# Stacked attention rows: four rows a channel in scratch memory, loaded by one transfer a side in lines of 2 KB

## The chip, the cores and the metric

The kernel runs on one NeuronCore of a Trainium2 chip. The metric is the device time of one execution in microseconds (us). Before the change the median of three runs is 694.81 us (693.26 to 694.91).

## What is computed

A decoder layer over x of 4 batches x 512 tokens x 256 channels, in float32. Only the first part is touched by the change:

```
x = layernorm(x + causal self-attention(x))     # 16 heads of 16 channels, weights 256 x 256
x = layernorm(x + cross-attention(x, ctx))      # 16 heads of 64 channels, 64 context rows a batch
x = layernorm(x + experts(x))                   # 8 experts, top 2, 256 -> 1024 -> 256
```

Self-attention: q = x Wq + bq, k = x Wk + bk, scores = q k / 4 with a causal mask, softmax, times v, times Wo, plus bo.

## The kernel before

**Precision by stacking.** Matmuls take float16. To keep float32 precision q and k are each split into a high and a low part (`qk[:, hl]`), and q k is formed as high x high + high x low + low x high. For that each channel is stacked as three rows of the contraction: `PARTS` says which part (0 high, 1 low) stands in row m on the q side and on the k side. A head has 16 channels, so 48 rows. Heads go in 8 pairs; the even head of a pair lies in partitions 0 to 47 and the odd one in partitions 64 to 111 of `qs` and `ks` (128 partitions x 8 pairs x 512 tokens). Row 48 (and 112) of `qs` holds minus the row maximum of the scores against ones in `ks`, so the score matmul (64 rows, `ROWS`) comes out with the maximum taken off; the rest of the 64 rows is zero in `qs`.

**Who fills the stacks.** For batch 0 TensorE stamps the rows out of `qk` with a 0/1 matrix `stamp` (step `st`, L926), and ScalarE evicts them (L618, L619). For batches 1, 2 and 3 the stacks go through scratch memory in HBM: step `store` (L437) writes six transfers of 256 KB, one for each side and row m, each a 1 KB line (one channel, 512 tokens) per descriptor. Step `stack` (L448) reads it back with four transfers of 384 KB: for each of `qs` and `ks` and each half of a pair 48 partitions x 8 pairs, again in lines of 1 KB, with the 8 lines of one partition 96 KB apart. Each batch has its own region of scratch. `qs` and `ks` have two buffers, batch b uses b % 2.

**Order.** All engines walk one handwritten list of steps, `ORDER`, in this order, each taking the steps that are its own; inside a batch the numbers are b:n. SyncE (SP) issues all these transfers from one queue. For batch b: `ql:b:1` (the low part of k is done) lets `store:b:0` go; `stack:b:0` waits for `qk_stored` and for the last score matmul of batch b-2; `m:b:0` on TensorE waits for `stack_in`. Steps `m:b:0` to `m:b:21` compute all scores once (L225, with the causal mask added by L230) for VectorE to take row maxima (L240); then `mT` and `max` bring the maxima into `qs` (L456), and `s:b:n` (L1035) computes the scores again for the exponentials (L681, ScalarE), `w` the sums with v (L1049), `ct`, `ct.n`, `cx`, `o` the projection, with VectorE's `cx.l` (L720), `o.d` (L817, then moments at L727 and L731), GpSimd's `r` (L559, L562) and VectorE's `n` (L828) for the layernorm. The `m` steps of batch b+1 are interleaved with the `s` and `w` steps of batch b and with the cross-attention (`xa`, `S`, `T`, `O`) of batch b. The part of the list around the second load reads:

```
o:0:0 o.d:0:0 stack:2:0 r:0:0 s:1:3 o:0:1 o.d:0:1 m:2:0 r:0:1 vw:0:0 w:1:0 ax:0:0 n:0:0 s:1:4 m:2:1 n:0:1 x1b:0:0 w:1:1 m:2:2 xa:0:0
```

Steps `A.s` and `VW.s` store products of the cross-attention's weights (`stage`) in scratch, also from SP's queue; `fold_done` waits for all of them, on ScalarE and VectorE ahead of `cx:0:0`, on SP ahead of the loads of `a_x` (L481) and `vw` (L488), 1 MB each.

Of the kernel before, what the change touches and what calls it, by code (L numbers as in the profile page):

```python
# [61 lines left out]
XS = 16.0  # L62
QS = 4.0
NEG = -60000.0
STACK = 3 * HD
PARTS = ((0, 0, 1), (0, 1, 0))
STORES, LOADS = 6, 4
ROWS = 64

# [118 lines left out]
class Tally:  # L190
# [3 lines left out]

    def upto(self, *step):
        return self.place[step]


def flat(ap):
# [44 lines left out]
def attention_block(nc, ctx, dram, keep):  # L244
# [100 lines left out]

    def kinds_of(x, hl):

        at = [m for m in range(3) if PARTS[x][m] == hl]
        step = at[1] - at[0] if len(at) > 1 else 1
        return stamp[:, x, hl, :].rearrange("p (r e) -> p r e", r=2)[:, :, 0:STACK].rearrange(  # L350
            "p r (d m) -> p r d m", m=3)[:, :, :, at[0]:at[-1] + 1:step], len(at)

    def fold_done(eng):

# [18 lines left out]
    def diagonal(n, hl, par):  # L373

        rows, pairs = slice(64 * par, 64 * par + 64), slice(n % 2 * 4, n % 2 * 4 + 4)
        return rows, v_diag[rows, hl, pairs, :, par, :].rearrange("p k b n -> p (k b) n")

    def half_of(n, hl):
        return pT[:, n // 2 % 2, hl, n % 2 * 4:n % 2 * 4 + 4, :].rearrange("p k q -> p (k q)")
# [10 lines left out]
    @block.sync  # L390
    def _(sp):
        def tokens(b, dst, done):
            sp.dma_start(dst[:, :, :], dram["x"][b * S:b * S + S, :]
                         .rearrange("(t p) d -> p t d", p=128)).then_inc(done, 16)

        tokens(0, x_tok, x_in)
        for n, w in enumerate(("Wq", "Wk")):
            sp.dma_start(w_f[:, n, :, :], dram[w].rearrange("(c p) n -> p c n", p=128)).then_inc(w_in[0], 16)
        sp.dma_start(qk_bias[:, 0, :], dram["bq"]).then_inc(b_in, 16)
        sp.dma_start(qk_bias[:, 1, :], dram["bk"]).then_inc(b_in, 16)  # L400
        for n, w in enumerate(("Wv", "Wo")):
            sp.dma_start(w_f[:, 2 + n, :, :], dram[w].rearrange("(c p) n -> p c n", p=128)).then_inc(w_in[1], 16)

        def load_rest():
            rows = dram["cond"].rearrange("(t p) d -> p t d", p=128)
            sp.dma_start(cond[:, :, 0, :], rows[:, :, 0:128]).then_inc(c_in, 16)
            for par in range(2):
                sp.dma_start(cond[:, :, 1, 64 * par:64 * par + 64], rows[:, :, 128:DCOND]).then_inc(c_in, 16)
            for n, w in enumerate(("w_k", "w_v")):
                sp.dma_start(wkv_f[:, n, :], dram[w][0:128, :]).then_inc(wkv_in[n], 16)  # L410
                sp.dma_start(wkv_f[64 * n:64 * n + 64, 2, :], dram[w][128:DCOND, :]).then_inc(wkv_in[2], 16)
            for n, bias in enumerate(("bo", "bv", "b_out")):
                sp.dma_start(b_rows[:, n, :], dram[bias].partition_broadcast(128)).then_inc(r_in, 16)
            sp.dma_start(wq_f[:, :, :], dram["w_q"].rearrange("(c p) n -> p c n", p=128)).then_inc(wq_in, 16)
            sp.dma_start(wout_f[:, :, :], dram["w_out"].rearrange("(k p) n -> p k n", p=128)).then_inc(wo_in, 16)
            sp.dma_start(wg_f[:, :, :], dram["WgT"]).then_inc(wg_in, 16)

        for kind, b, n in STEPS:
            if kind == "x_in":
                filled(sp, g, "xT", b - 1, 1)  # L420
                tokens(b, x_tok, x_in)
                if b == 1:
                    load_rest()
            elif kind == "xr_in":
                if b == 0:
                    sp.wait_ge(wout_lo, 1)
                    for m in range(4):
                        freed_slot(sp, r, "kv", m, 0)
                else:
                    freed_slot(sp, g, "o", b - 1, 1)  # L430
                tokens(b, x_res, xr_in)
            elif kind == "store":
                sp.wait_ge(qlo_done, 2 * b + 2)
                rows = dram["qk"][b * 6 * D:(b + 1) * 6 * D, :].rearrange("(t c p m) s -> t m p c s", t=2, c=DC, m=3)
                for t, parts in enumerate(PARTS):
                    for m, hl in enumerate(parts):
                        sp.dma_start(rows[t, m, :, :, :], qk[:, hl, 2 * t:2 * t + 2, :]).then_inc(qk_stored, 16)  # L437
            elif kind == "stack":

                sp.wait_ge(qk_stored, STORES * 16 * b)  # L440
                if b < 2:
                    sp.wait_ge(stack_set, 2)
                else:
                    filled(sp, r, "s", b - 2, STAGE - 1)
                rows = dram["qk"][b * 6 * D:(b + 1) * 6 * D, :].rearrange("(t p r e) s -> t r e p s", t=2, r=2, e=STACK)
                for t, dst in enumerate((qs[b % 2], ks[b % 2])):
                    for par in range(2):
                        sp.dma_start(dst[64 * par:64 * par + STACK, :, :], rows[t, par, :, :, :]).then_inc(stack_in[b % 2], 16)  # L448
            elif kind == "max":

                freed_slot(sp, g, "mT", b, 0)
                if b >= 2:
                    sp.wait_ge(stack_in[b % 2], (b + 1) // 2 * LOADS * 16)
                for par in range(2):
                    row = 64 * par + STACK
                    sp.dma_start(qs[b % 2][row:row + 1, :, :], neg_maxT[par * PAIRS:(par + 1) * PAIRS, :]  # L456
                                 ).then_inc(max_in, 16)
            elif kind == "A.s":
                use = use_of["A", b]
                sp.wait_ge(a_lo, b + 1)  # L460
                c, q = b // 4, b % 4
                dst = dram["ax"].rearrange("(b p) (l c n) -> p l b c n", p=128, l=2, c=DC)[
                    :, :, :, c, q * 256:q * 256 + 256]
                src = stage[:, use % 2, :, :].rearrange("p l (b n) -> p l b n", b=NB)
                for hl in range(2):
                    sp.dma_start(dst[:, hl, :, :], src[:, hl, :, :]).then_inc(staged[use % 2], 16)
            elif kind == "VW.s":
                use = use_of["VW", b]
                freed_slot(sp, r, "VW", b, 0)
                half = b % 2  # L470
                dst = dram["vw"][b // 2 * 128:b // 2 * 128 + 128, :].rearrange("p (l h n) -> p l h n", l=2, h=2)[
                    :, :, half:half + 1, :]
                src = stage[:, use % 2, :, :].rearrange("p l (h n) -> p l h n", h=1)
                for hl in range(2):
                    sp.dma_start(dst[:, hl, :, :], src[:, hl, :, :]).then_inc(staged[use % 2], 16)
            elif kind == "ax":
                if b == 0:
                    fold_done(sp)
                else:
                    filled(sp, g, "S", b - 1, 2 * NQ - 1)  # L480
                sp.dma_start(a_x[:, :, :, :].rearrange("p l c n -> p (l c n)"),  # L481
                             dram["ax"][b * 128:b * 128 + 128, :]).then_inc(ax_in, 16)
            elif kind == "vw":
                if b == 0:
                    fold_done(sp)
                else:
                    filled(sp, g, "O", b - 1, NQ - 1)
                sp.dma_start(vw[:, :, :, :].rearrange("p l k n -> p (l k n)"),  # L488
                             dram["vw"][b * 128:b * 128 + 128, :]).then_inc(vw_in, 16)
        sp.wait_ge(wg_lo, 1)  # L490
# [91 lines left out]
    def _(act):  # L582
# [7 lines left out]
        for kind, b, n in STEPS:  # L590
# [7 lines left out]
            elif kind == "q":  # L598
                if b == 0 and n == 0:
                    act.wait_ge(bias_done, 2)  # L600
                if n == 0 and b > 0:
                    positive(act, qk_stored, STORES * 16 * (b - 1))
                bank, empty = filled(act, r, kind, b, n)

                if b > 0:
# [100 lines left out]
    def _(dve):  # L706
# [16 lines left out]
        def moments(n, buf):  # L723
# [6 lines left out]
            for t in tiles:  # L730
# [3 lines left out]
        dve.wait_ge(consts, 1)  # L734
        V.tensor_reduce(squares[:, :], ident[:, :].rearrange("p (j e) -> p e j", e=32), AX.X, ALU.add
                        ).then_inc(squares_sum, 1)
        V.tensor_reduce(pads[:, :], ident[:, :].rearrange("p (r e) -> p r e", r=2)[:, :, STACK:], AX.XY, ALU.add
                        ).then_inc(pads_set, 1)
        dve.wait_ge(squares_sum, 1)
        dve.wait_ge(stamp_clear, 1)  # L740
# [145 lines left out]
    def _(pe):  # L886
# [15 lines left out]
        for kind, b, n in STEPS:  # L902
# [14 lines left out]
            elif kind == "st":  # L917
# [2 lines left out]
                    pe.wait_ge(stamp_set, 4)  # L920
                    pe.wait_ge(qlo_done, 2)
                bank, full = opened(r, kind, b, n)
                rows = slice(32 * (n % 4), 32 * (n % 4) + 32)
                for x in range(2):
                    for hl in range(2):
                        last = M.matmul(bank[:, x, :], stamp[rows, x, hl, :], qk[rows, hl, 2 * x + n // 4, :],  # L926
                                        start=hl == 0, stop=hl == 1)
                last.then_inc(full, 1)
            elif kind == "v":
# [97 lines left out]
            elif kind == "s":  # L1027
# [1 line left out]
                    pe.wait_ge(max_in, 32 * b + 32)  # L1029
                bank, full = opened(r, kind, b, n)  # L1030
                for x, j, at in SCORES[n % ITEMS]:
                    p = 2 * (n // ITEMS) + x
                    for par in range(2):
                        rows = slice(64 * par, 64 * par + ROWS)
                        last = M.matmul(bank[:, par, at:at + S - 128 * j], ks[b % 2][rows, p, 128 * j:128 * j + 128],  # L1035
# [830 lines left out]
```

## Time and profile before

| | |
|---|---|
| median of 3 runs | 694.81 us |
| the profiled execution's own time | 693.73 us |
| its span | 692.0 us |
| mean granted TensorE clock | 0.969 |
| busy: PE, DVE, ACT, POOL | 603.4, 530.1, 407.9, 303.2 us |
| attention block | up to about 412 us of the span |
| transfers from SP's queue | 92.55 MB |

PE is TensorE's matmuls, PEld its weight loads (they overlap), DVE is VectorE, ACT ScalarE, POOL GpSimd, SPq the queue of SyncE. "L225" is a line of the kernel. "idle before <-releaser" says how long an engine sat idle just ahead of an instruction and whose work ended that wait. A busy PE is not a PE at its peak, since ends of matmuls are modelled; idle time of an engine that is not the one everything waits for costs nothing.

### The profile page before, as it was taken

Reading aid. Unit: us, or ns where it says so; the run is one execution under the profiler, and the core shown is the slowest. Engines: PE = TensorE matmul, PEld = TensorE weight load, DVE = VectorE, ACT = ScalarE, POOL = GpSimd, SP = SyncE. Lnnn points to the kernel's source line nnn. Section 1 sums busy time; section 2 is a strip of 40 time slices with the busy share of each in tenths; the row PEclk is TensorE's granted clock in tenths of the full one; section 3 lists DMA queues with packets and bytes.
Section 4 is the critical chain, followed back from the end, with each engine's and each line's share of the span. In section 5 each row is a group of like instructions: output and inputs, shape, how many; then the busy total and the mean of one; then the engine's idle time right before and its main releaser. Section 6 shows DMA issues by size and latency. Waiting matters only on the chain. (4 is left out here: it accounts for less than half of the span.)

```text
span 692.0 us, 13570 instructions
## 1 busy us (share of the span) xinstructions
PE 603.4 (87%) x5232; PEld 414.6 (60%) x5232; DVE 530.1 (77%) x930; ACT 407.9 (59%) x622; POOL 303.2 (44%) x363
## 2 busy tenths in 40 slices
PE   5989688887999799898987853899999999999984
PEld 2435344453444535454654543698989989988963
DVE  4687576528877688877757779699999999999725
ACT  3655578763466344455651313388888988987613
POOL 9311255545356244625452434325464642662223
PEclk9999999999999999999999995699999999999998
DMA  7407454394002900111020017578888779786264
GB/s 229 143 1 176 100 153 153 104 254 163 1 1 92 218 28 14 48 64 31 1 94 30 0 35 239 169 260 267 300 288 283 264 267 290 264 279 208 92 227 161
DMA packets 70992, 103.65 MB, mean 150 GB/s; under 512 B 4848, under 2 KB 56776, under 8 KB 69904
## 3 DMA queue, kind: packets, MB, share of 16 engines
q1 hardware_dynamic: 67184, 92.55, 42.3%
q0 software_dynamic: 3744, 10.23, 4.2%
q8 instruction: 42, 0.69, 0.4%
q14 instruction: 22, 0.18, 0.1%
HBM read 80.28 MB, written 22.41 MB: 148 GB/s over the span
## 5 line engine op out<-in xcount | busy, mean ns | idle before, releaser
L240 DVE TENSOR_REDUCE rowmax<-M 128x1 f32<-128x512 f32 (+3 forms) x176 | 104.6, 636 | 37.6 <-PE M L230 35.5
L681 ACT ACTIVATE probs<-R 128x1024 f32<-128x1024 f32 x80 | 80.4, 1028 | 51.2 <-PE R L1035 50.9
L213 PE MATMUL HB<-xT,w 128*128 128x256 f16 (+1 forms) x1104 | 107.8, 258 | 0.3 <-DVE xT L1615 0.3
L1770 PE MATMUL YB<-w,h 128*128 128x256 f16 x936 | 105.9, 273 | 0.1
L213 PEld LDWEIGHTS HB<-xT,w 128*128 128x128 f16 x1104 | 94.8, 98 | 11.2 <-DVE xT L1615 1.7
L1770 PEld LDWEIGHTS YB<-w,h 128*128 128x128 f16 x936 | 91.4, 98 | 10.8 <-issue 0.4
L543 POOL TENSOR_SCALAR_AFFINE_SELECT probs<-probs 128x256 f32<-128x256 f32 x128 | 49.6, 407 | 97.4 <-ACT probs L681 96.9
L1467 ACT ACTIVATE hf<-HB,b 128x256 f32<-128x256 f32 (+1 forms) x184 | 69.9, 445 | 37.0 <-PE HB L213 35.5
L1388 POOL DMA_INDIRECT scratch_ys<-y,dst x39 | 41.9, 1075 | 98.2 <-ACT y L1447 93.0
L1380 POOL DMA_INDIRECT xg<-scratch_xs,src x39 | 62.4, 1601 | 26.6 <-issue 10.9
L1642 DVE SCALAR_TENSOR_TENSOR h<-hf,h 128x512 f16<-128x512 f32 (+1 forms) x92 | 56.6, 616 | 3.2
L1627 DVE SCALAR_TENSOR_TENSOR w<-w2f,w 128x2048 f16<-128x2048 f32 x23 | 52.6, 2288 | 8.3 <-ACT w L1453 8.3
L225 PE MATMUL M<-ks,qs 48*128 48x384 f16 (+3 forms) x256 | 33.8, 303 | 21.0 <-DVE rowmax L240 13.7
L1620 DVE SCALAR_TENSOR_TENSOR w<-w1f,w 128x2048 f16<-128x2048 f32 x22 | 50.3, 2285 | 1.0 <-ACT w L1438 0.6
L213 PE MATMUL M<-a_x,x1T 128*128 128x512 f16 x192 | 45.6, 380 | 5.0 <-DVE logits L874 1.6
L213 PE MATMUL M<-vw,pT 128*128 128x256 f16 x384 | 44.6, 273 | 3.2 <-DVE pT L720 3.1
L1438 ACT ACTIVATE w<-w1f 128x2048 f16<-128x2048 f32 x23 | 44.2, 1920 | 4.1 <-DMA w1f<-in_W 4.1
L1453 ACT ACTIVATE w<-w2f 128x2048 f16<-128x2048 f32 x23 | 44.3, 1927 | 2.2 <-DMA w2f<-in_W 2.2
L1049 PE MATMUL PV<-probs,v_aug 128*32 128x256 f32 (+3 forms) x512 | 44.2, 444 | 0.0
L213 PEld LDWEIGHTS M<-vw,pT 128*128 128x128 f16 x384 | 36.7, 98 | 10.9 <-DVE pT L720 4.3
L578 POOL TENSOR_TENSOR e_x<-e_x,xinv 128x1024 f32<-128x1024 f32 x16 | 30.4, 1902 | 22.4 <-DVE xinv L852 22.3
L225 PEld LDWEIGHTS M<-ks,qs 48*128 48x128 f16 x256 | 12.1, 95 | 43.8 <-issue 23.8
(272 smaller groups left out, 1071.7 us busy)
## 6 DMA issues: line engine op xcount, KB each, us to landing
w1f<-in_W SPq DMA_DIRECT2D x23, 1024.0 KB, 7.6
w2f<-in_W SPq DMA_DIRECT2D x23, 1024.0 KB, 6.0
scratch_qk<-qk SPq DMA_DIRECT2D x18, 256.0 KB, 3.0
scratch_ax<-stage SPq DMA_DIRECT2D x16, 256.0 KB, 2.5
scratch_vw<-stage SPq DMA_DIRECT2D x16, 256.0 KB, 2.9
vw<-scratch_vw SPq DMA_DIRECT2D x4, 1024.0 KB, 7.4
a_x<-scratch_ax SPq DMA_DIRECT2D x4, 1024.0 KB, 9.5
parts<-scratch_ys SPq DMA_DIRECT2D x8, 512.0 KB, 8.6
```

The source lines that it names most:

```text
L213: last = nc.tensor.matmul(out, left(a, k), right(b, k), start=(k == 0 and m == 0), stop=(k == n - 1 and m == 2))
L225: nc.tensor.matmul(banks[par][:, p * wide:p * wide + wide], qs[rows, p0 + p, t * 128:t * 128 + 128], ks[rows, p0 + p, 0:wide], start=p == ...
L240: return nc.vector.tensor_reduce(rowmax[:, t, par * PAIRS + p0:par * PAIRS + p0 + pairs], bank[:, 0:pairs * wide].rearrange("p (n w) -> p ...
L543: last = P.affine_select(out=diag, in_=diag, compare_op=ALU.is_ge, fill=0.0, base=0, pattern=[[0, 2], [1, 128]], channel_multiplier=-1)
L681: A.activation(probs[:, n % RING, :, :], bank[:, :, :], ACT.Exp, scale=1.0 / (QS * QS)).then_inc(empty, 1)
L1380: pool.indirect_dma_start(out=xg[:, n % 2, t, :], out_offset=None, in_=dram["xs"], in_offset=bass.IndirectOffsetOnAxis(src[:, at:at + 1], ...
L1453: A.activation(w2[:, q, 0, :, :].rearrange("p m d -> p (m d)"), w2f[:, q, :, :].rearrange("p m d -> p (m d)"), ACT.Copy, scale=WS).then_in ...
L1467: last = A.activation(hf[:, 2 * b + m, 0:width(n)], HB[b][:, m, 0:width(n)], ACT.Gelu, bias=b1[:, 2 * b + m, WORK[n]:WORK[n] + 1], scale=1 ...
L1620: V.scalar_tensor_tensor(w1[:, q, 1, :, :].rearrange("p c f -> p (c f)"), w1f[:, q, :, :].rearrange("p c f -> p (c f)"), WS, w1[:, q, 0, : ...
L1627: V.scalar_tensor_tensor(w2[:, q, 1, :, :].rearrange("p m d -> p (m d)"), w2f[:, q, :, :].rearrange("p m d -> p (m d)"), WS, w2[:, q, 0, : ...
L1642: V.scalar_tensor_tensor(h[:, q, 1, pair, at], hf[:, pair, at], XS, h[:, q, 0, pair, at], ALU.mult, ALU.subtract).then_inc(h_split, 1)
L1770: last = M.matmul(YB[q][:, t, :], h[:, q, a, m, t * 128:t * 128 + 128], w2[:, q, b, m, :], start=((m, a, b) == (0, 0, 0)), stop=((m, a) == ...
```

## The change

Each channel now has four rows in scratch, of which the fourth is a filler (zeros for q, ones for k, written once ahead of the first store from the set buffers `qs[1]` and `ks[1]`). `STACK` and `ROWS` are 64, so a head fills its half of the partitions. The two chunks c of 128 channels lie side by side, so that a line is 2 KB. One region of scratch serves all batches, so a store waits until the load of the batch before has landed. A store is four transfers (two of them write a part twice, from a source with a step of zero), a load is two transfers of 1 MB, over all 128 partitions, with the 4 lines of one partition 256 KB apart. Pairs take another order (`place_of`), and minus the maximum goes to row 3 (and 67). The stamps and pads of batch 0 follow the new order of rows.

```diff
-STACK = 3 * HD
+PARTED = 4
+STACK = PARTED * HD
-STORES, LOADS = 6, 4
-ROWS = 64
+STORES, LOADS = 4, 2
+ROWS = STACK
...
+def places(x, hl):
+    at = [m for m in range(3) if PARTS[x][m] == hl]
+    return slice(at[0], at[-1] + 1, at[-1] - at[0] or 1), len(at)
...
+    def place_of(pair):
+        return pair % (PAIRS // DC) * DC + pair // (PAIRS // DC)
...
+        stack_rows = dram["qk"].rearrange("(t p m c) s -> t p m (c s)", t=2, m=PARTED, c=DC)
+        stack_lines = dram["qk"].rearrange("(t q e c) s -> t e q (c s)", t=2, e=128, c=DC)
...
                 sp.wait_ge(qlo_done, 2 * b + 2)
-                rows = dram["qk"][b * 6 * D:(b + 1) * 6 * D, :].rearrange("(t c p m) s -> t m p c s", t=2, c=DC, m=3)
-                for t, parts in enumerate(PARTS):
-                    for m, hl in enumerate(parts):
-                        sp.dma_start(rows[t, m, :, :, :], qk[:, hl, 2 * t:2 * t + 2, :]).then_inc(qk_stored, 16)
+                if b == 1:
+                    sp.wait_ge(stack_set, 2)
+                    for t, fill in enumerate((qs[1], ks[1])):
+                        sp.dma_start(stack_rows[t, :, 3, :], flat(fill[:, 0:DC, :])).then_inc(qk_stored, 16)
+                else:
+                    sp.wait_ge(stack_in[(b - 1) % 2], b // 2 * LOADS * 16)
+                for t in range(2):
+                    for hl in range(2):
+                        where, many = places(t, hl)
+                        sp.dma_start(stack_rows[t, :, where, :], flat(qk[:, hl, 2 * t:2 * t + 2, :]).unsqueeze(1)
+                                     .to_broadcast([128, many, DC * S])).then_inc(qk_stored, 16)
...
-                sp.wait_ge(qk_stored, STORES * 16 * b)
+                sp.wait_ge(qk_stored, (2 + STORES * b) * 16)
...
-                rows = dram["qk"][b * 6 * D:(b + 1) * 6 * D, :].rearrange("(t p r e) s -> t r e p s", t=2, r=2, e=STACK)
                 for t, dst in enumerate((qs[b % 2], ks[b % 2])):
-                    for par in range(2):
-                        sp.dma_start(dst[64 * par:64 * par + STACK, :, :], rows[t, par, :, :, :]).then_inc(stack_in[b % 2], 16)
+                    sp.dma_start(dst[:, :, :].rearrange("e (q c) s -> e q (c s)", c=DC), stack_lines[t, :, :, :]
+                                 ).then_inc(stack_in[b % 2], 16)
...
-                    row = 64 * par + STACK
+                    row = 64 * par + PARTED - 1
...
-                    positive(act, qk_stored, STORES * 16 * (b - 1))
+                    positive(act, qk_stored, (2 + STORES * (b - 1)) * 16 if b > 1 else 0)
...
-                rows = slice(32 * (n % 4), 32 * (n % 4) + 32)
+                rows, c = slice(32 * (n // DC), 32 * (n // DC) + 32), n % DC
...
-                    p = 2 * (n // ITEMS) + x
+                    p = place_of(2 * (n // ITEMS) + x)
```

## Rows read from the trace of the kernel before

**Rows 1.** Busy time by stretch: us, engines (instructions), clock, DMA share, GB/s.
```profile
159.00:216.00 57.00, 52.59 (x418) 24.98 (x418) 46.63 (x84) 30.32 (x41) 27.32 (x35) 1.00 0.09 37
239.00:300.00 61.00, 55.51 (x458) 27.08 (x456) 52.70 (x95) 28.97 (x36) 28.60 (x41) 0.97 0.13 48
```

**Rows 2.** Waits of the whole span: us in total, times, longest.
```profile
PE M L225 <- DVE rowmax L240: 13.7, 22, 1.0
PE M L225 <- DMA ks<-scratch_qk: 6.5, 2, 3.9
```

**Rows 3.** Timeline ahead of and behind the load of batch 2: start, duration.
```profile
146.88 0.96 SPq L448 DMA_DIRECT2D qs<-scratch_qk  x2
158.09 0.25 DVE L731 BATCH_NORM_AGGREGATE meanvar<-stats 128x2 f32<-128x6 f32 x2
158.92 0.40 PE L225 MATMUL M<-ks,qs 48*128 48x128 f16 x8 [2.57 <-DMA ks<-scratch_qk]
159.67 1.29 DVE L240 TENSOR_REDUCE rowmax<-M 128x4 f32<-128x512 f32 x2 [1.34 <-PE M L230]
```

**Rows 4.** Timeline around the load of batch 3.
```profile
226.20 0.90 SPq L448 DMA_DIRECT2D qs<-scratch_qk  x2
236.22 0.25 DVE L731 BATCH_NORM_AGGREGATE meanvar<-stats 128x2 f32<-128x6 f32 x2
238.74 0.40 PE L225 MATMUL M<-ks,qs 48*128 48x128 f16 x8 [3.95 <-DMA ks<-scratch_qk]
239.49 1.29 DVE L240 TENSOR_REDUCE rowmax<-M 128x4 f32<-128x512 f32 x2 [3.02 <-PE M L230]
241.73 1.29 DVE L240 TENSOR_REDUCE rowmax<-M 128x4 f32<-128x512 f32 x2 [0.30 <-PE M L230]
244.29 1.29 DVE L240 TENSOR_REDUCE rowmax<-M 128x2 f32<-128x512 f32 x2 [0.62 <-PE M L230]
```

**Rows 5.** Stretches behind that wait (columns as Rows 1): the granted clock.
```profile
239.00:240.00 1.00, 1.00 (x12) 0.27 (x8) 0.51 (x1) 0.00 (x0) 0.00 (x0) 0.73 1.03 434
241.00:242.00 1.00, 1.00 (x6) 0.13 (x2) 0.70 (x3) 1.00 (x2) 0.47 (x2) 0.50 0.95 393
242.00:243.00 1.00, 1.00 (x9) 0.20 (x8) 1.00 (x3) 0.28 (x1) 0.85 (x3) 0.57 1.01 363
```

**Rows 6.** Pace of transfers by stretch (columns as Rows 1, the last is GB/s).
```profile
148.40:156.00 7.60, 5.43 (x42) 3.38 (x43) 2.75 (x6) 3.60 (x5) 3.67 (x5) 1.00 1.10 201
227.20:236.00 8.80, 7.59 (x67) 6.03 (x65) 5.67 (x16) 3.67 (x4) 2.18 (x5) 1.00 1.09 178
22.00:24.00 2.00, 1.52 (x9) 0.42 (x7) 1.38 (x2) 1.17 (x2) 0.00 (x0) 1.00 1.07 382
238.00:241.00 3.00, 2.26 (x26) 1.21 (x26) 1.51 (x3) 0.66 (x1) 0.00 (x0) 0.74 0.99 418
138.20:142.50 4.30, 4.30 (x46) 2.14 (x46) 0.69 (x3) 3.60 (x7) 2.70 (x3) 1.00 1.07 352
147.00:148.20 1.20, 1.10 (x10) 0.86 (x8) 0.27 (x2) 1.20 (x3) 0.00 (x0) 1.00 1.17 372
```

**Rows 7.** Issues in 226 to 228: queue, count, KB each, median us to landing.
```profile
qs<-scratch_qk SPq DMA_DIRECT2D x2, 384.0 KB, 5.6
ks<-scratch_qk SPq DMA_DIRECT2D x2, 384.0 KB, 9.7
```

**Rows 8.** Timeline of SP's stores and of what waits for the last of them.
```profile
137.89 3.82 SPq L437 DMA_DIRECT2D scratch_qk<-qk  x6
144.13 1.22 DVE L720 SCALAR_TENSOR_TENSOR stage<-R,stage 128x1024 f16<-128x1024 f32 x1 [4.67 <-ACT stage L667]
145.79 1.00 SPq L475 DMA_DIRECT2D scratch_vw<-stage  x2
151.02 1.08 ACT L588 ACTIVATE ctxT<-M 128x512 f16<-128x512 f32 x2 [2.04 <-DMA scratch_vw<-stage]
```

**Rows 9.** Timeline of batch 1: load issued, first matmul on it.
```profile
63.76 0.99 SPq L448 DMA_DIRECT2D ks<-scratch_qk  x2
82.56 0.32 PEld L225 LDWEIGHTS M<-ks,qs 48*128 48x128 f16 x8
```

**Rows 10.** Matmuls on the stacks by form, 48 and 64 rows: count, busy, mean ns.
```profile
L225 PE MATMUL M<-ks,qs 48*128 48x512 f16 x64 | 12.8, 382 | 5.9 <-DVE rowmax L240 5.9
L1035 PE MATMUL R<-qs,ks 64*128 64x512 f16 x64 | 12.3, 386 | 2.3 <-DVE stage L720 1.4 <-ACT w_f L663 0.5 <-ACT v_next L623 0.2
```

More of the change, by code:

```diff
@@ L346, in kinds_of @@
     def kinds_of(x, hl):
[L348 to L351, printed above, removed]
+        where, many = places(x, hl)
+        return stamp[:, x, hl, :].rearrange("p (r d m) -> p r d m", r=2, m=PARTED)[:, :, :, where], many
     def fold_done(eng):
@@ L736, in _ @@
                         ).then_inc(squares_sum, 1)
-        V.tensor_reduce(pads[:, :], ident[:, :].rearrange("p (r e) -> p r e", r=2)[:, :, STACK:], AX.XY, ALU.add
+        V.tensor_reduce(pads[:, :], ident[:, :].rearrange("p (d m) -> p d m", m=PARTED)[:, :, PARTED - 1:], AX.XY, ALU.add
                         ).then_inc(pads_set, 1)
@@ L922, in _ @@
                 bank, full = opened(r, kind, b, n)
-                rows = slice(32 * (n % 4), 32 * (n % 4) + 32)
+                rows, c = slice(32 * (n // DC), 32 * (n // DC) + 32), n % DC
                 for x in range(2):
                     for hl in range(2):
-                        last = M.matmul(bank[:, x, :], stamp[rows, x, hl, :], qk[rows, hl, 2 * x + n // 4, :],
+                        last = M.matmul(bank[:, x, :], stamp[rows, x, hl, :], qk[rows, hl, 2 * x + c, :],
                                         start=hl == 0, stop=hl == 1)
@@ L1858 @@
     dram["out"] = nc.dram_tensor("out", (T, D), F32, kind="ExternalOutput").ap()
-    for name, shape, dt in (("qk", (NB * 6 * D, S), F16), ("ax", (NB * 128, 2 * DC * XA), F16),
+    for name, shape, dt in (("qk", (2 * PARTED * D, S), F16), ("ax", (NB * 128, 2 * DC * XA), F16),
                             ("vw", (NB * 128, 2 * PAIRS * D), F16),
```

## Prediction

> **What bounds the kernel now.** I read the busy times by stretch first. Between the load of batch 2 and that of batch 3, and behind the latter, TensorE is busy 52.59 of 57 us and 55.51 of 61 us, VectorE 46.63 and 52.70 [rows 1]. TensorE works through one list in order, so what it idles there moves the end unless another engine holds it up anyway. The list of waits names the two causes: 13.7 us in 22 small waits for row maxima, and 6.5 us in only two waits for the transfer into `ks` [rows 2]. The timeline shows both: 2.57 us ahead of `m:2:0` [rows 3] and 3.95 us ahead of `m:3:0` [rows 4]. VectorE sits idle behind them, but less, as it still has the moments of a layernorm to do: 1.34 us and 3.02 us [rows 3, 4]. The clock rows show one more cost: after the 3.95 us idle the granted clock falls from 1.0 to one half, from 2.4 to 1.2 GHz, for about 3.4 us (0.54 of the 239th, the next two, and 0.86 of the 242nd) [rows 5]. Nothing of the sort follows on the 2.57 us one.
>
> Why is the load late? It moves 4 x 384 KB = 1.57 MB. With all DMA engines busy (share 1.09 to 1.10) the queue makes only 201 and 178 GB/s in the two stretches that it fills, while 1 KB lines of `w_out` to 128 partitions, 128 KB apart, go at 382, and the 8 KB lines of `a_x` and `vw` at 418 [rows 6]. So 1 KB lines are not slow as such. What sets this load apart is that a transfer reaches 48 partitions of one half.
>
> **The load, changed.** Two transfers over 128 partitions in 2 KB lines carry 2 x 1,048,576 B = 2.10 MB, a third more. At the pace of the nearest row of like shape, 382 GB/s, that is 5.5 us; at 418 it is 5.0; at the old 178 it is 11.8. I take 5.5.
>
> Batch 3: the first transfer is issued at 226.20 and the data flow from 227.2. At 178 GB/s 1.57 MB last 8.8 us, to 236.0. The last `ks` transfer lands just before TensorE starts at 238.74, at about 238.65: that leaves a tail of 2.6 us for what `a_x` and `vw` take of the engines and for the completion. The median landing of the two `ks` transfers, 9.7 us against 5.6 for `qs`, shows the queue growing [rows 4, 6, 7]. New: 227.2 + 5.5 + 2.6 = 235.3. TensorE is there at 238.74 - 3.95 = 234.79 and waits 0.5 us at most. VectorE ends its moments at 236.47, and needs the result of `m:3:0` 0.75 us after its start (239.49 against 238.74), so at 235.3 + 0.75 = 236.05 it is in time. VectorE gains its whole idle time, 3.02 us.
>
> Batch 2: stores are still in the queue when the load is issued at 146.88 (372 GB/s from 147.0 to 148.2), so I start at 148.3: 148.3 + 5.5 + 2.6 = 156.4, against 156.35 when TensorE is there and 158.34 - 0.75 = 157.6 when VectorE needs it [rows 3, 6]. It gains 1.34 us.
>
> Which of the engines' gains goes on? Ahead of `xa`, TensorE needs both halves of the layernorm (`n`), and these stand on VectorE behind the row maxima of `m:b:0` and `m:b:1`. So VectorE's gain passes, and the rest of TensorE's becomes waits for row maxima. I take 1.34 + 3.02 = 4.36 us. The upper end is TensorE's own 2.57 + 3.95 = 6.52 us.
>
> **The clock.** With TensorE idle for 0.5 us in place of 3.95 I expect no fall there. VectorE waited 0.30 and 0.62 us for matmuls at the low clock [rows 4]: 0.92 us, which I take. The upper end is half of the 3.4 us at low clock, 1.7 us; the lower is none, if the fall comes somewhere else.
>
> **The stores.** Six transfers become four, of the same 1.57 MB, in 768 lines of 2 KB instead of 1,536 of 1 KB. They go at 352 GB/s now [rows 6], 4.5 us; at the 372 of the stores of `vw`, which have lines of 2 KB, 4.2. SP spends 3.82 us on six issues, 0.64 each, so about 1.3 less. That matters at one place: `VW.s:7:0` is issued at 145.79, 0.44 after VectorE is done at 145.35, and ScalarE waits 2.04 us for its landing ahead of `ctxT`, on whose path the layernorm of batch 0 stands [rows 8]. I take 0.4 us, between -0.5 (2 KB lines of the load get among the last stores) and 1.9 (TensorE's wait for `ctxT` gone). The wait added ahead of the store, for the load of the batch before, would hold up SP's queue, that is `max`, `A.s`, `VW.s` and `stack` behind it, and with them `s` and `m` of TensorE. It costs nothing: the loads of batches 1 and 2 are in use from 82.56 and 158.92, the stores of 2 and 3 come at 137.89 and 58 us after the second [rows 3, 8, 9]. The two filler transfers (0.52 MB, 1.5 us at 352) delay only the load of batch 1, issued by 64.75 and landed some 10 us later, if it takes what the `ks` transfers of rows 7 take, but wanted at 82.56 [rows 9]: over 7 us of cover, and the load gets shorter.
>
> **Matmuls.** `m` goes from 48 to 64 rows. 48 rows take 382 ns and 64 rows 386 at 512 columns [rows 10]; the 4 ns may be a matter of place. 64 x 4 ns = 0.26 us, bounds 0 and 0.3: I take 0.1. The order of pairs, row 3 for the maximum, stamps and pads change addresses only: nothing, with bounds of 0.2 either way, as the instructions keep their shapes.
>
> **Sum.** -4.36 - 0.92 - 0.4 + 0.1 = -5.6 us. Against the profiled execution's own time of 693.73: 688.1. Against the median, 694.81, it would be 689.2; the two differ by 1.1 us, which is the spread of the runs. I predict 688.6 us, which is 5.6 below 694.2; the rivals' times are from 694.2 too. The part from 300 us on is left as it is; it starts earlier.
>
> **Rivals.**
> 1. *The source is what is slow* (slower). The load reads back what was just written, in lines far apart. If this sets 178 to 201 GB/s, and not the 48 partitions, then 2.10 MB take 11.8 us in batch 3 and 10.4 in batch 2: 3.0 and 2.6 us longer than 1.57 MB now. Both waits grow by that, and the one of 5.2 us at `m:2:0` brings a low clock too, some 1 us: +6.6, 701 us. It decides below 2.10 / 8.8 = 238 GB/s, the pace at which the new load lasts as long as the old. For it: the data come from scratch, and lines 96 KB apart become lines 256 KB apart. Against it: lines 128 KB apart at 382, and `vw` and `a_x`, also from scratch, at 418 [rows 6]. [...]
> 2. *Half a gain* (no change). The pace comes out near 280 GB/s, between 178 and 382: 7.5 us. Batch 3 lands at 227.2 + 7.5 + 2.6 = 237.3 and gains 1.35, batch 2 at 158.4 gains 0.5, and the low clock may stay: 1.9 us or less, 692.3.
> 3. *TensorE's whole wait comes back.* If row maxima are not what holds it afterwards, 6.52 + 1.7 and 0.4 of the stores make -8.6: 685.6. Against it: 13.7 us of waits for row maxima as it is [rows 2].
>
> **How the numbers follow.** Forecast 0.66, rival 3 0.12, rival 2 0.12, rival 1 0.10. A run is told from no change beyond 0.3%, 2.1 us. The forecast and rival 3 are faster, and a little of rival 2: 0.79. Same: 0.13. Slower: 0.08, as a mild form of rival 1 stays within 2.1 us. The forecast's own range is 686 to 691. The whole range is 685.3 to 693.5: it holds rivals 2 and 3 and leaves out rival 1.
>
> **What would show it.** The list of waits has no wait for `ks` above 1 us. The two loads show 350 GB/s or more and land within 10 us of issue; at 238 or less rival 1 holds. The clock stays at 1.0 behind `m:3:0`. `xa:0:0` starts some 1.7 us and `xa:1:0` some 5.5 us earlier than now, while the small waits for row maxima grow by 1 to 2 us. If the load is early and the end is not, my step from VectorE's idle time to the end was wrong.

## The result, and the profile after

| | median us | runs | lowest, highest |
|---|---|---|---|
| before | 697.14 | 12 | 693.26, 711.63 |
| after | 689.73 | 12 | 685.24, 695.78 |

The ratio is 0.9891, 95% interval 0.9859 to 0.9923: the kernel is faster by 7.6 us (5.4 to 9.8). The forecast of 688.6 us was a gain of 5.6, a ratio of 0.992, inside the interval, near its upper end. Ratios, here and below, leave out the runs that lie over 1.5% above the fastest of their kernel, so they differ a little from those of the medians.

The profiled execution of the changed kernel has a span of 694.0 us (own time 695.78), 2 us longer than that of before. In it, as in some of those below, TensorE was granted a lower clock in early stretches that the change doesn't touch, so I compare distances between steps and not the spans. The stretch 20 to 40 us shows it, first of before, then of after: span, then PE, PEld, DVE, ACT, POOL busy (instructions), clock, DMA share, GB/s.

```profile
20.00:40.00 20.00, 18.83 (x124) 8.63 (x122) 14.22 (x23) 12.27 (x20) 3.06 (x7) 1.00 0.23 86
```

```profile
20.00:40.00 20.00, 19.49 (x104) 8.93 (x103) 11.70 (x19) 10.40 (x17) 3.08 (x7) 0.83 0.20 71
```

The timeline of the kernel after, from the stores of batch 2 to its load and then around the load of batch 3 (start, duration; the idle time ahead in brackets):

```profile
143.12 2.74 SPq L454 DMA_DIRECT2D scratch_qk<-qk  x4
147.90 0.94 SPq L483 DMA_DIRECT2D scratch_ax<-stage  x2
149.30 1.23 DVE L737 SCALAR_TENSOR_TENSOR stage<-R,stage 128x1024 f16<-128x1024 f32 x1 [4.67 <-ACT stage L684]
150.56 0.81 SPq L492 DMA_DIRECT2D scratch_vw<-stage  x2
151.47 0.40 SPq L464 DMA_DIRECT2D qs<-scratch_qk  x1
155.30 1.09 ACT L605 ACTIVATE ctxT<-M 128x512 f16<-128x512 f32 x2 [1.15 <-DMA scratch_vw<-stage]
160.57 0.40 PE L232 MATMUL M<-ks,qs 64*128 64x128 f16 x8
162.54 1.25 DVE L247 TENSOR_REDUCE rowmax<-M 128x4 f32<-128x512 f32 x2
166.50 1.32 PE L915 MATMUL M<-ident,x 128*128 128x128 f32 x8 [0.43 <-DVE x L845]
...
228.95 0.38 SPq L464 DMA_DIRECT2D qs<-scratch_qk  x1
238.25 0.40 PE L232 MATMUL M<-ks,qs 64*128 64x128 f16 x8 [0.71 <-DMA ks<-scratch_qk]
239.13 1.26 DVE L247 TENSOR_REDUCE rowmax<-M 128x4 f32<-128x512 f32 x2
244.23 0.63 PE L915 MATMUL M<-ident,x 128*128 128x128 f32 x4
```

The waits of 2.57 and 3.95 us for `ks` [rows 3, 4] are none and 0.71 now; VectorE's idle times of 1.34 and 3.02 ahead of the row maxima have no bracket left. The list of waits says the same of the whole span: 6.5 us in two waits became 0.7 in one, and the small waits for row maxima grew from 13.7 us in 22 to 14.4 in 24 [rows 2].

```profile
PE M L232 <- DVE rowmax L247: 14.4, 24, 1.0
PE M L232 <- DMA ks<-scratch_qk: 0.7, 1, 0.7
```

The load's pace and landing (a stretch as above, then the DMA issues of the whole span: count, KB each, median us to landing): 396 GB/s where 178 were, with the clock at 1.0 [rows 6]. `ks` lands in 8.5 us, the median of the three loads, instead of 9.3; in batch 3 it is 8.8 instead of 9.7 [rows 7], with a third more bytes.

```profile
232.00:236.00 4.00, 4.00 (x37) 3.21 (x36) 2.33 (x8) 1.36 (x3) 0.88 (x2) 1.00 1.04 396
```

```profile
qs<-scratch_qk SPq DMA_DIRECT2D x3, 1024.0 KB, 5.7
ks<-scratch_qk SPq DMA_DIRECT2D x3, 1024.0 KB, 8.5
```

Now the kernels before and after and five variants of after side by side: the span cut at six steps, with the length of each part in us. "Load 2" runs from the first issue of `store:2:0` to `xa:0:0`, "load 3" from the first issue of `stack:3:0` to `xa:1:0`; `XB` is the first matmul of the expert block.

| kernel | to store:1:0 | to store:2:0 | load 2 | to stack:3:0 | load 3 | to XB | to the end |
|---|---|---|---|---|---|---|---|
| before | 56.59 | 81.30 | 25.86 | 62.45 | 19.65 | 166.48 | 279.67 |
| after | 60.05 | 83.07 | 23.38 | 62.45 | 15.28 | 169.49 | 280.28 |
| c_after | 57.38 | 83.09 | 23.75 | 62.48 | 15.30 | 166.57 | 280.43 |
| e5_six_stores | 56.11 | 81.10 | 23.17 | 62.40 | 15.49 | 166.50 | 278.43 |
| e8_every_second | 56.36 | 81.26 | 23.39 | 62.51 | 15.63 | 166.50 | 279.65 |
| e1_halves | 56.59 | 81.33 | 27.76 | 62.73 | 21.10 | 169.83 | 278.06 |
| e9_halves_short | 55.83 | 81.07 | 28.34 | 62.47 | 20.91 | 166.47 | 280.11 |

The part between the loads repeats within 0.4 us in these seven, and only the load parts move with the change: 2.48 and 4.37 us in the profile of after. The row of before is one profile. What after loses lies in the first two parts (5.2 us) and the sixth (3.0).

### The profile page after: what moved, and what is told of

The parts are those of the page before. It is cut to its first block and busy times, and to the rows that moved or that the text cites. A ratio compares the mean times of both kernels' runs of the same rounds, so it can differ in the third digit from the quotient of the medians.

```text
span 694.0 us, 13563 instructions
## 1 busy us (share of the span) xinstructions
PE 610.5 (88%) x5232; PEld 416.0 (60%) x5232; DVE 529.4 (76%) x930; ACT 408.0 (59%) x622; POOL 305.2 (44%) x363
## 5 line engine op out<-in xcount | busy, mean ns | idle before, releaser
L1397 POOL DMA_INDIRECT xg<-scratch_xs,src x39 | 64.3, 1648 | 27.1 <-PE XB L1774 11.1
L220 PE MATMUL M<-a_x,x1T 128*128 128x512 f16 x192 | 47.2, 389 | 4.8 <-DVE logits L891 1.6
L232 PE MATMUL M<-ks,qs 64*128 64x384 f16 (+3 forms) x256 | 34.6, 309 | 16.0 <-DVE rowmax L247 14.4
L605 ACT ACTIVATE pT<-M 128x512 f16<-128x512 f32 x32 | 18.2, 595 | 32.8 <-PE M L1108 32.8
```

The costliest lines, as they stand in the source:

```text
L220: last = nc.tensor.matmul(out, left(a, k), right(b, k), start=(k == 0 and m == 0), stop=(k == n - 1 and m == 2))
L1397: pool.indirect_dma_start(out=xg[:, n % 2, t, :], out_offset=None, in_=dram["xs"], in_offset=bass.IndirectOffsetOnAxis(src[:, at:at + 1], ...
```

## The experiments

My theory: the old load is slow since each transfer reaches partitions of one half only; once it is quick, VectorE's idle time and the low clock are what comes back. Rivals: the longer lines or fewer transfers make it quick; part of the gain is the stores'. Every edit is against the kernel after, unless it says before. Ratios are to runs of the kernel before on the same chip, whose medians were 699.8 to 700.3 us.

### c_after: the kernel after as it is

> The changed kernel as it is, for a second profile beside the kernel before on one chip. My theory (the load over 128 partitions is what counts, and VectorE's idle time plus the clock passes to the end): ratio 0.985 to 0.993, the wait for ks ahead of m:3:0 under 1 us, the load issued to landed in under 9 us, no low clock within 5 us behind m:3:0. The rival (row maxima take most of it back): ratio 0.995 or more.

Ratio 0.9854 (0.9792 to 0.9916), median 688.24. Timeline and stretch again:

```profile
226.70 0.38 SPq L464 DMA_DIRECT2D qs<-scratch_qk  x1
236.02 0.40 PE L232 MATMUL M<-ks,qs 64*128 64x128 f16 x8 [0.77 <-DMA ks<-scratch_qk]
242.00 0.63 PE L915 MATMUL M<-ident,x 128*128 128x128 f32 x4
```

```profile
229.50:233.50 4.00, 4.00 (x37) 3.22 (x36) 2.32 (x8) 1.42 (x2) 0.88 (x2) 1.00 1.05 400
```

`m:3:0` starts 9.32 us after the issue, as in the first profile (9.30); the pace repeats too. What I expected of the theory came but for the landing: `ks` lands 8.9 us after its own issue and 9.3 after the first, where I had under 9.

### e1_halves: the load in halves

```diff
-STORES, LOADS = 4, 2
+STORES, LOADS = 4, 4
-                    sp.dma_start(dst[:, :, :].rearrange(...), stack_lines[t, :, :, :]
-                                 ).then_inc(stack_in[b % 2], 16)
+                    for half in (slice(0, 64), slice(64, 128)):
+                        sp.dma_start(dst[half, :, :].rearrange(...), stack_lines[t, half, :, :]
+                                     ).then_inc(stack_in[b % 2], 16)
```

> The changed kernel with its load in four transfers, each over 64 partitions (0 to 63, then 64 to 127 of qs, then of ks), still in lines of 2 KB, the same 2.10 MB. Theory 'partitions' (a transfer that reaches only one half of the partitions is slow, 178 to 201 GB/s, whatever its lines): pace 180 to 230 GB/s, last ks transfer lands 12 to 14 us after the first issue, waits for ks of 3 us or more at m:2:0 and m:3:0, the gain gone or turned to a loss, ratio 0.997 to 1.008. Rival 'lines' (1 KB lines were slow, 2 KB are not): pace 380 or more, as the changed kernel, ratio 0.987 to 0.993.

Ratio 1.0016 (0.998 to 1.0051), median 699.41: the same bytes in the same 2 KB lines, and the whole gain is gone.

```profile
158.66 0.61 PE L232 MATMUL M<-ks,qs 64*128 64x128 f16 x8 [3.57 <-DMA ks<-scratch_qk]
242.12 0.61 PE L232 MATMUL M<-ks,qs 64*128 64x128 f16 x8 [5.18 <-DMA ks<-scratch_qk]
249.51 0.60 PE L916 MATMUL M<-ident,x 128*128 128x128 f32 x4
```

```profile
230.00:238.00 8.00, 6.95 (x61) 5.46 (x59) 5.52 (x16) 3.66 (x4) 2.19 (x5) 1.00 1.00 222
243.00:244.00 1.00, 1.00 (x6) 0.21 (x6) 0.69 (x2) 0.00 (x0) 0.00 (x0) 0.50 1.02 434
```

The pace is 222 GB/s with the DMA share at 1.00 all the same, and behind the 5.18 us wait the clock is at 0.50, 1.2 GHz. The last stretch holds the reads of `a_x` and `vw` over all partitions, which go at 434 a few us later. So the queue isn't slow, and the source is the one that c_after reads at 400.

### e8_every_second: four loads of 64 partitions, but of both halves

```diff
-                    for half in (slice(0, 64), slice(64, 128)):
+                    for half in (slice(0, 128, 2), slice(1, 128, 2)):
```

(against e1_halves)

> The changed kernel with its load in four transfers of 64 partitions and 2 KB lines, as e1_halves, but one takes the even and the other the odd partitions of all 128. Theory 'where the partitions lie' (a transfer into one half of SBUF is held to half the pace, and the number of partitions and of transfers does not count): pace 350 to 400 GB/s, waits for ks under 1.5 us, ratio 0.985 to 0.993. Rival 'how many' (64 partitions a transfer are too few to fill the DMA engines): pace near 222 GB/s as in e1_halves, waits for ks of 3 us or more, ratio 0.998 or more.

Ratio 0.9894 (0.9852 to 0.9937), median 688.77. Count, size and lines of the transfers are those of e1_halves; only which 64 partitions one reaches differs, and some 10 us are back. The two waits are 1.33 and 1.13 us:

```profile
233.17 0.40 PE L232 MATMUL M<-ks,qs 64*128 64x128 f16 x8 [1.13 <-DMA ks<-scratch_qk]
```

```profile
226.00:232.00 6.00, 6.00 (x53) 4.61 (x50) 4.11 (x14) 2.65 (x3) 1.29 (x3) 1.00 1.03 365
```

### e2_short_lines and e9_halves_short: lines of 1 KB

```diff
+                    for c in range(DC):
+                        sp.dma_start(<dst, chunk c>, stack_lines[t, :, :, c * S:c * S + S]
+                                     ).then_inc(stack_in[b % 2], 16)
```

e2 has these four transfers over 128 partitions; e9 splits them by halves as well, which makes eight.

> The changed kernel with its load in four transfers, each over 128 partitions but for one of the two chunks, so in lines of 1 KB, the same 2.10 MB in 2,048 lines. Theory 'partitions': pace 350 to 390 GB/s, waits for ks under 1.2 us, ratio 0.987 to 0.994. Rival 'lines': pace near 200 GB/s, waits for ks above 3 us, ratio 0.998 or more.

> The changed kernel with its load in eight transfers, each over one half of the partitions and one chunk: 64 partitions, lines of 1 KB, the same 2.10 MB. It is the fourth corner of a square: 128 partitions and 2 KB 400 GB/s, 128 and 1 KB 343, 64 of one half and 2 KB 222. If the short lines cost their own part on top, the pace is 180 to 200 GB/s and the load of batch 3 lands 12.5 to 14 us after its first issue, xa:1:0 comes 21.5 us or more after stack:3:0 (21.1 with 2 KB lines), ratio 1.000 to 1.010. If the halves alone set the pace, it stays at 215 or more.

e2: ratio 0.9865 (0.9815 to 0.9914), median 689.15. e9: 1.0052 (1.0005 to 1.0099), median 699.43. The load's stretch and the wait ahead of `m:3:0`, first of e2, then of e9:

```profile
230.00:234.00 4.00, 4.00 (x37) 3.20 (x34) 2.33 (x8) 1.48 (x2) 0.89 (x2) 1.00 1.05 343
```

```profile
237.49 0.40 PE L232 MATMUL M<-ks,qs 64*128 64x128 f16 x8 [1.68 <-DMA ks<-scratch_qk]
```

```profile
230.00:238.00 8.00, 6.28 (x55) 4.81 (x53) 5.89 (x18) 3.67 (x4) 2.58 (x6) 1.00 1.13 227
```

```profile
241.65 0.61 PE L232 MATMUL M<-ks,qs 64*128 64x128 f16 x8 [5.38 <-DMA ks<-scratch_qk]
```

Over all partitions 1 KB lines go at 343 GB/s, 14% under 2 KB lines; I had expected 350 to 390, and waits under 1.2 us. The wait ahead of `m:3:0` grows from 0.77 to 1.68 us, and load 3 takes 16.27 us, 1.0 more than in c_after, too little for the ratio to tell. In halves the line's length changes nothing (227 against 222).

### e11_halves_48: 48 partitions of each half

```diff
-                    for half in (slice(0, 64), slice(64, 128)):
+                    for half in (slice(0, 48), slice(64, 112)):
```

(against e1_halves; the other 16 partitions of each half aren't loaded and keep what the stacks held)

> e1_halves with 48 of each half's 64 partitions (0 to 47 and 64 to 111), lines of 2 KB, 1.57 MB; the other 32 partitions keep what the buffers held, so the last heads' rows are stale. The kernel before makes 178 to 201 GB/s on these partitions in lines of 1 KB, 64 of a half make 222. If the 48 are what costs the rest, the pace is 170 to 200 GB/s and xa:1:0 comes 19 to 20.5 us after stack:3:0, as before (19.7), ratio 0.994 to 1.004. If the 96 KB between the lines or something else in the old layout did it, the pace is 215 or more and the load of 1.57 MB lands 2 us sooner than before, ratio 0.990 to 0.997.

Ratio 0.994 (0.989 to 0.9989), median 696.92.

```profile
240.00:248.00 8.00, 5.63 (x49) 4.23 (x47) 5.28 (x17) 3.35 (x4) 3.11 (x8) 1.00 1.09 181
```

```profile
249.64 0.40 PE L232 MATMUL M<-ks,qs 64*128 64x128 f16 x8 [4.00 <-DMA ks<-scratch_qk]
```

This is the old load but for the lines of 2 KB and the 256 KB between them, and it has the old pace (181 against 178), the old wait (4.00 against 3.95) and the old part "load 3" (19.69 against 19.65). So from 48 partitions of a half to 64 the pace goes from 181 to 222, and from a half to the whole from 222 to 400. The ratio is better than these parts explain: they come to +0.3 us, and the interval, a gain of 0.8 to 7.7 us, leaves out no change. The ratio of c_after is 3.7 us better than its two load parts as well, while that of e9 agrees with them. I can't say what else got quicker here, and leave that open.

### e3_before_thin: the kernel before without most of its load

```diff
-                        sp.dma_start(dst[64 * par:64 * par + STACK, :, :], rows[t, par, :, :, :])...
+                        sp.dma_start(dst[64 * par:64 * par + STACK, 0:1, :], rows[t, par, :, 0:1, :])...
```

(one of the eight pairs is loaded, the others keep old rows)

> The kernel before, whose loads carry only pair 0 of the eight (48 KB instead of 384 KB a transfer); the other pairs of batches 1 to 3 keep what the buffers held, so part of the computation is on stale rows. It takes the cost of the late load out and leaves the stores as they were. My sum for the loads alone, 1.34 + 3.02 + 0.92 = 5.3 us, expects ratio 0.990 to 0.994 and xa:1:0 some 5 us earlier against store:2:0; it stands for the part of the changed kernel's gain that is not from the stores. If the stores carry most of the gain, ratio 0.997 or more; if TensorE's whole wait comes back, 0.987 to 0.989.

Ratio 0.9887 (0.9835 to 0.9938), median 690.54. That is below the 0.990 to 0.994 that I expected of my sum, in the band that I gave to TensorE's whole wait; the interval holds both, so the steps have to decide. The stores, the rows and the matmuls are those of before, and the gain is as large as that of the change:

```profile
238.38 0.84 SPq L448 DMA_DIRECT2D qs<-scratch_qk  x2
246.81 0.39 PE L225 MATMUL M<-ks,qs 48*128 48x128 f16 x8
249.37 0.40 PE L225 MATMUL M<-ks,qs 48*128 48x128 f16 x8 [0.89 <-DVE rowmax L240]
253.79 0.63 PE L898 MATMUL M<-ident,x 128*128 128x128 f32 x4
```

`m:3:0` waits for nothing, 8.43 us after the issue, and yet `xa:1:0` comes 15.41 us after it, as in after (15.28): the 0.9 us that TensorE is earlier here goes into a wait for a row maximum.

Load 2 takes 23.88 us, 1.98 less than before, but that isn't like for like. From 150 to 160 us the granted clock was 0.83, where before had 1.00 behind its `store:2:0`, and VectorE's last product `stage` ahead of `VW.s:7:0` starts 7.81 us after the issue of `store:2:0` instead of 6.24. ScalarE's `ctxT` has no bracket: the wait of 2.04 us for the stores of `vw` [rows 8] is gone, with the old stores.

```profile
150.00:160.00 10.00, 8.77 (x78) 5.15 (x79) 3.19 (x6) 6.93 (x10) 4.43 (x7) 0.83 0.77 253
```

```profile
159.86 1.23 DVE L720 SCALAR_TENSOR_TENSOR stage<-R,stage 128x1024 f16<-128x1024 f32 x1 [5.12 <-ACT stage L667]
164.56 1.14 ACT L588 ACTIVATE ctxT<-M 128x512 f16<-128x512 f32 x2
```

Counted from the start of that product (144.13 us before, 149.30 after, 159.86 here), where the low clock lies behind, the steps come after, in us:

| kernel | `ctxT` | first row maximum of batch 2 | `xa:0:0` |
|---|---|---|---|
| before | 6.89 | 15.54 | 19.62 |
| after | 6.00 | 13.24 | 17.20 |
| c_after | 6.35 | 13.58 | 17.57 |
| e5_six_stores | 5.95 | 13.18 | 16.99 |
| e10_before_fill_all | 6.48 | 15.14 | 19.22 |
| e3_before_thin | 4.70 | 12.11 | 16.07 |
| e6_after_thin | 5.29 | 12.53 | 16.49 |

e10, further down, is the kernel before up to the load of batch 3, and its clock was low ahead of the product as well (it starts 7.76 us after the issue of `store:2:0`). Its whole load makes `ctxT` wait 1.62 us, and without most of the load batch 2 gains 3.15 us against it, 3.55 against before. In each of the other kernels the row maximum gains VectorE's idle time, 1.34, and what `ctxT` gains, within 0.1 us; in e10 that idle time is still there.

### e6_after_thin: the kernel after with a quarter of its load

```diff
-                    sp.dma_start(dst[:, :, :].rearrange(...), stack_lines[t, :, :, :]
+                    sp.dma_start(dst[:, 0:DC, :].rearrange(...), stack_lines[t, :, 0:1, :]
```

(one of four lines is loaded, the rest keeps old rows)

> The changed kernel whose loads carry one of four lines of a partition (256 KB instead of 1 MB a transfer); the other pairs of batches 1 to 3 keep what the buffers held. It shows what is left of the load's cost: 0.8 us of wait for ks at m:3:0, of which VectorE feels little. I expect the changed kernel's ratio less 0 to 0.0015, 0.984 to 0.992. If traffic of the load still delays a_x and vw or the stores of vw, it is faster by 2 us or more, ratio 0.983 or less.

Ratio 0.9882 (0.9819 to 0.9944), median 686.17. Load 2 takes 22.67 and load 3 15.42 us, against 23.17 to 23.75 and 15.28 to 15.49 with the whole load. In batch 3 nothing is left to gain from the load; in batch 2 it may be 0.5 to 1 us, and there `ctxT` waits 0.44 us for the stores of `vw` instead of 1.1 to 1.5.

### e5_six_stores: six stores instead of four

```diff
-                    for hl in range(2):
-                        where, many = places(t, hl)
-                        sp.dma_start(stack_rows[t, :, where, :], <broadcast source>)...
+                    for m, hl in enumerate(PARTS[t]):
+                        sp.dma_start(stack_rows[t, :, m, :], flat(qk[:, hl, 2 * t:2 * t + 2, :]))...
```

> The changed kernel with six stores of 256 KB again (each part written by a transfer of its own, no source with a step of zero), in the same 2 KB lines. If the fewer issues on SP are what brings ctxT of batch 0 forward, SP takes 3.8 us instead of 2.8 for the store, and ScalarE's wait for the stores of vw goes from some 1.2 to 2 us: ratio 0.5 to 1 us worse than the changed kernel, 0.987 to 0.995. If the lines of 2 KB are, nothing changes against it.

Ratio 0.9894 (0.9849 to 0.9939), median 688.43. The issues and what waits behind them:

```profile
137.21 3.40 SPq L453 DMA_DIRECT2D scratch_qk<-qk  x6
142.45 0.99 SPq L482 DMA_DIRECT2D scratch_ax<-stage  x2
149.34 1.08 ACT L604 ACTIVATE ctxT<-M 128x512 f16<-128x512 f32 x2 [1.10 <-DMA scratch_vw<-stage]
```

SP is busy for 3.40 us instead of 2.74 and `ctxT` waits 1.10, as with four stores (1.15, and 1.50 in c_after), against 2.04 before [rows 8]. So the number of issues is not what shortened this wait. Nor is it what frees SP's queue: the two issues of `A.s` behind the stores take 0.99 us here and 0.94 in after, against 2.19 before:

```profile
143.55 2.19 SPq L466 DMA_DIRECT2D scratch_ax<-stage  x2
```

The stores of `vw` are issued 0.02 and 0.03 us after VectorE is done, against 0.44 [rows 8]. The lines of 2 KB and the load changed as well. A load that is slow as before doesn't bring the wait back: e1, e9 and e11 have 0.82, 0.57 and 1.17 us. That speaks for the lines of 2 KB, but I didn't try them alone.

### e4_before_fill and e10_before_fill_all: the wait kept, TensorE kept busy

```diff
-cx:1:1 ... stack:3:0 r:1:1 m:3:0 ax:1:0
+cx:1:1 ... stack:3:0 r:1:1 idle:240:12 m:3:0 ax:1:0
```

(before, with 12 matmuls on the identity, 19 in e10, where TensorE waits for batch 3's load; nobody reads them)

> The kernel before with twelve idle matmuls of 512 columns (some 2.6 us) put into TensorE's wait of 3.95 us ahead of m:3:0; nothing else is changed, and the wait for the load stays. If the low clock behind that wait costs what I put down, VectorE's 0.30 and 0.62 us and up to 1.7 us of TensorE, the clock stays at 1.0 there and xa:1:0 comes 0.9 to 1.7 us earlier against stack:3:0; ratio 0.997 to 0.999, perhaps not to be told from 1. If the low clock costs nothing, xa:1:0 does not move.

> The kernel before with nineteen idle matmuls (some 4.3 us) in the wait ahead of m:3:0, so that TensorE idles under 0.5 us there. In e4_before_fill twelve left a wait of 1.9 us and the clock fell all the same. If an idle TensorE is what takes the clock down, it stays at 1.0 from stack:3:0 to xa:1:0, which comes 18.3 to 19.3 us after it instead of 19.7, and the ratio is 0.997 to 1.000. If the clock falls here too, the term of 0.92 us in my sum was not due to the wait.

e4: ratio 1.0041 (1.0 to 1.0082), median 700.59. e10: 1.0016 (0.9965 to 1.0067), median 701.09. Timeline and clock, first e4, then e10:

```profile
254.87 2.76 PE L943 MATMUL R<-ident 128*128 128x512 f16 x12
259.53 0.40 PE L225 MATMUL M<-ks,qs 48*128 48x128 f16 x8 [1.90 <-DMA ks<-scratch_qk]
```

```profile
262.00:263.00 1.00, 1.00 (x6) 0.20 (x8) 0.91 (x3) 0.78 (x1) 0.88 (x3) 0.50 0.89 362
```

```profile
232.76 0.89 SPq L448 DMA_DIRECT2D qs<-scratch_qk  x2
241.28 4.28 PE L943 MATMUL R<-ident 128*128 128x512 f16 x19
245.49 0.40 PE L225 MATMUL M<-ks,qs 48*128 48x128 f16 x8
246.25 1.29 DVE L240 TENSOR_REDUCE rowmax<-M 128x4 f32<-128x512 f32 x2 [3.21 <-PE M L230]
251.47 0.63 PE L898 MATMUL M<-ident,x 128*128 128x128 f32 x4
```

```profile
247.00:248.00 1.00, 0.92 (x14) 0.42 (x17) 1.00 (x3) 1.00 (x2) 0.02 (x1) 1.00 1.06 451
```

e4 didn't do what it was for: a wait of 1.90 us was left, and the clock still fell to one half behind it. I had expected `xa:1:0` 0.9 to 1.7 us earlier; load 3 takes 20.59 us, 0.94 more than before, 0.64 of it since `ks` came later (`m:3:0` starts 13.18 us after the issue, against 12.54). In e10 TensorE has no gap, the clock stays at 1.0, and load 3 takes 18.71 us against 19.65, 0.94 less. The clock is worth a little more than that, since the first row maximum starts 13.49 us after the issue here and 13.29 before [rows 4]: from it to `xa:1:0` there are 5.22 us against 6.36, 1.14 less. The ratio can't show so little; it lies above the 0.997 to 1.000 that I expected, and its interval holds them.

## Why the prediction was right

**The load's pace.** Forecast 382 GB/s, by the nearest row with 1 KB lines to 128 partitions; measured 396 and 400. The reason is settled by e1, e8, e2 and e9: one half of the partitions gets about half the pace, in lines of either length, and 64 partitions spread over both halves get 365. The Trainium skill ("SBUF — State Buffer", Door 1: The DMA port swizzle) says that the 64 partitions of one half reach 8 of the 16 ports on which DMA enters, and those of both halves all 16; the traces agree, with 222 against 365 to 400 GB/s. It also says that partitions 0 to 31 reach as many ports as 0 to 63 do; that 48 get less than 64 here (181 against 222) stays open.

**Rival 1, the slow source,** is refuted: reads of lines 256 KB apart go at 400 GB/s, and e1_halves, with the same source, at 222. **Rival 2,** 280 GB/s, falls with it.

**Landing.** Forecast 9.1 us after the issue and at most 0.5 us of waiting; measured 9.3 and 0.7 to 0.8. The tail is longer than the 2.6 us that I kept: 2.10 MB at 396 GB/s take 5.3 us, and with 1.0 from the issue to the first data some 3.0 are left, an estimate.

**From VectorE's idle time to the end.** Forecast 3.02 + 0.92 = 3.94 us for batch 3, and not TensorE's 3.95 and the clock on top. Load 3 is 4.0 to 4.4 us shorter in after, c_after, e5 and e8, and e3 without stores or rows changed gives 4.24. VectorE's first row maximum starts 10.15 to 10.18 us after the issue in after, c_after and e3, against 13.29: 3.1 us. The kernel after alone can't tell this from TensorE's account, as `m:3:0` starts 3.24 us earlier. e3 and e6 can: `m:3:0` starts 8.43 us after the issue in both, 0.9 sooner than in after, and `xa:1:0` no sooner, since the earlier matmuls end in a wait for a row maximum. So rival 3 is not what happened in batch 3; the small waits grew by 0.7 us, though, not by 1 to 2.

**The clock.** Forecast 0.92; measured by e10, in one profile, 0.94 at `xa:1:0` and 1.14 from the first row maximum on.

**Batch 2** is the term that was too small. Forecast 1.34 and 0.4 for the stores, 1.74; load 2 is 2.1 to 2.7 us shorter. The 1.34 came back whole: VectorE has no idle time left ahead of the row maxima. The term that was mis-sized is `ctxT`, put down at 0.4: counted from VectorE's product it starts 0.5 to 0.9 us sooner (table under e3), and 1.2 in e8. Of this 0.4 is the earlier issue of the stores of `vw`, but not by fewer issues, as e5 has it with six. The rest, 0.1 to 0.8, is their quicker landing. I had given the load no part in that, and e3 shows that it has one: with the old stores and most of the load gone `ctxT` starts 1.78 us sooner than in e10. How the gain of the changed kernel splits between its stores and its load stays open.

**The sum.** The two load parts are 6.5 to 6.9 us shorter, against 5.6 forecast and 7.6 (5.4 to 9.8) timed. The matmuls' 0.1 can't be told: between `xa:1:0` and `XB` there are 166.48 us before and 166.50 to 166.57 after where the clock is undisturbed, so it is below 0.1 there. `xa:0:0` and `xa:1:0` were to come 1.7 and 5.5 us earlier; from the issue of `store:2:0` they come 2.1 to 2.7 and 6.4 to 6.9 earlier.

**Some luck.** The time, 689.73 against 688.6, came out nearer than the gain. The forecast started from 694.2, and the median of the twelve runs of before is 697.14, 2.9 higher; the medians differ by 7.4 and not by 5.6, 1.8 more. The two cancel in part.

The chance of 0.66 on the forecast rested on paces measured elsewhere in the same trace, and that was the right place to look. What I had not weighed is the spread from run to run, several us, which for a term of 0.4 or 0.9 us makes the distances in a profile the only instrument.

## What to carry to other kernels

Where a load fills all DMA engines (share 1.0) and yet moves half of what another in the same trace moves, look at which partitions one transfer reaches: both halves in one transfer, even with a third more bytes, beat halves one after the other. The gain of an earlier load is the idle time of the engine that is next to hold up the path, not of the one that waits longest, with what the clock loses behind the wait on top. A large load can also delay small stores that were issued just ahead of it, and what waits for them. Compare distances between the same steps before comparing spans.

## What the runs showed of the hardware that was not expected

- A full DMA share is no full pace: 178, 222 and 400 GB/s all go with a share between 1.00 and 1.10.
- With every second partition in one transfer and the others in the next, 64 partitions go at 365 GB/s, nearly as 128 do.
- With the load cut to an eighth (e3), ScalarE's wait for the stores of `vw`, which are issued 0.9 to 1.1 us ahead of the load, was gone; it is 2.04 us before and 1.62 in e10.
- TensorE's clock fell to one half behind a wait of 1.90 us (e4), although TensorE had been busy for all of the 11.3 us ahead of it. In the kernel before it didn't fall behind one of 2.57 us [rows 3], with 7.0 us busy of the 9.4 ahead. I can't say what tells them apart.
- The clock also falls in stretches without a long wait of TensorE (the longest from 285 to 300 us is 0.8), at other places in each execution. Of the kernel after, 290 to 300 us:

```profile
290.00:300.00 10.00, 8.70 (x66) 3.22 (x68) 8.13 (x16) 4.86 (x7) 2.77 (x7) 0.83 0.01 2
```

  Before had 1.00 in that stretch, and its profile is 3.0 us shorter in the part around it; runs of the same kernel spread over 685 to 696 us.
